# Routed token rows that carry their own token number and weights, in a mixture-of-experts stage on one core

## The chip, the cores and the metric

One core of a Trainium2 chip runs the whole kernel: a cross attention, a self attention and a mixture-of-experts block (MoE), one after the other. The metric is the device time of one execution in microseconds (us), the median of several runs.

Engines are named as in the profile: PE (TensorE), DVE (VectorE), ACT (ScalarE), POOL (GpSimd), SP (SyncE, which here only issues DMAs). An engine executes its own instructions in order, and a wait holds up everything behind it on that engine.

## The reference, cut to what matters

```python
# x: (8, 128, 512) after two attention blocks; E = 8 experts, F = 1024
def ffn(x, Wg, Wu, Wd, W1, W2):
    xt = x.reshape(1024, 512)
    probs = softmax(xt @ Wg)
    topv, topi = top_k(probs, 2)
    topv = topv / sum(topv, axis=-1)            # two weights per token
    cw = zeros((1024, 8)).at[arange(1024)[:, None], topi].set(topv)
    h = gelu(einsum('td,edf->tef', xt, Wu))
    y = einsum('tef,efd->ted', h, Wd)
    moe = einsum('ted,te->td', y, cw)
    return gelu(xt @ W1) @ W2 + moe
x = x + ffn(layernorm(x), ...)
```

Only two of the eight experts count for each token, so the kernel computes just those (2048 token and expert pairs instead of 8192).

## The kernel before, in words

The change lies in `experts()`, the last of three parts that run one after the other on all engines. Everything is float32, made of two or three passes of the faster fp32r format: a value is split into a rounded "high" part (by ACT) and a "low" rest (by DVE or POOL), and products of high and low parts are summed in PSUM.

**Tiles.** A tile is 128 rows of 512 numbers, multiplied by a pair of weight matrices (`up`, 512x1024, then GELU, then `down`, 1024x512). NT = 8 *shared* tiles (the tokens in their order, weights W1 and W2) come first. Tiles 0 to 3 of them are done in the self attention, tiles 4 to 7 in `experts()`. Then come the *routed* tiles, numbered from 8, expert after expert: each expert has the tokens that chose it, padded to whole tiles of 128. How many tiles an expert has is known only at run time (the table `first_i`); at most 31 tiles in all, and in this data 21 routed tiles, numbers 8 to 28.

**One tile** on PE, in `tile()`: 8 matmuls at each of L1728, L1732 and L1738 into `up_ps` (high x high, low x high, high x low); `turn_hidden(t, 0)` (4 transposes, L1716) as soon as ACT has made the first half of the GELU (L1799); `turn_next(t)`, the 4 transposes (L1693) of the *next* tile's rows; `turn_hidden(t, 1)`; then 8 matmuls at each of L1750, L1756 and L1760 into `down_ps`. For a shared tile the next rows are in `xn3` in SBUF; for a routed one `turn_next` first waits on `row_in`, for the DMA that fetches the row tile.

**The order of ACT's work** in `tile(t)`: two GELUs (L1799), two roundings of the transposed hidden values (L1802), the rounding of the next tile's transposed rows (`round_row`, L1785), then `load_row(t + 2)`, a DMA (L1781) of row tile t+2 from DRAM into the single buffer `row`. It can start because `rowT_done` says that the former contents of `row` have been transposed. At the start of an expert e the ACT program has `round_weights(e + 2)`, eight roundings (L1793) of the *following* expert's weights, before the GELUs of the expert's first tile.

**The order of DVE's work** in a routed tile: the low rests of the hidden values (L1848) and of the next rows (L1842); then a wait for `down_done`; then `target`, the token numbers of the tile's 128 rows (L1937), and `y`, the result times its weight (L1938), both from columns of `tag`. POOL adds `y` into the output by an indirect DMA at the rows `target` (L1646).

**Routing and scatter.** DVE finds the two experts, the weights and the slot of every token (a chain of small instructions in which each waits for the former by `link`, such as L1907; it ends with L1918, `slots_done`). Then POOL issues

- 16 indirect DMAs (8 tiles of tokens x 2 experts, L1656) that write each token's normalised row of 2048 bytes to its slot in `rows_dram`; they count on the semaphore `rows_sent`;
- 16 more (L1665) that write the pair (token number, weight), 8 bytes, to the same slot in `meta_dram`, which SP has filled with "no token, weight 0" from `pad`; they count on `added`.

Slots that no token takes must hold harmless rows: SP writes zeros from `wxo[:, 0, :]` to the 25 row tiles of `rows_dram` during the cross attention (L258 in `cross_attention`).

**Who waits for the scatter.** ACT, in `tile(NT - 2)` (tile 6), waits for `rows_sent` after `round_row(7)` and before `load_row(8)`; it then loads row tile 8, and row tile 9 in `tile(NT - 1)`. SP loads all of `meta_dram` into `tag` (L1611, `tags_in`) when `added` says that the small scatters have landed; DVE and POOL wait for `tags_in` before the routed tiles.

```python
            def tile(t, before_load=None):
                ...
                round_row(t + 1)
                if before_load:
                    before_load()
                if not isinstance(t, int) or t + 2 >= NT:
                    load_row(t + 2)
            ...
            tile(NT - 2, lambda: act.wait_ge(rows_sent, 16 * 2 * NT))
            tile(NT - 1)
```

SP's queue around this: the loads of expert 1's weights (`load_raw(2)`, 8 of 512 KB), the store of tile 6 and of tile 7, the load of `tag`, the loads of the next experts' weights.

Of the kernel before, what the change touches and what calls it, by code (L numbers as in the profile page):

```python
# [59 lines left out]
def cross_attention(nc, x_ap, ctx_ap, wq_ap, wk_ap, wv_ap, wxo_ap, q_dram, o_dram, rows_dram, wxo, wxo_in, stage, on,  # L60
# [5 lines left out]
    with ExitStack() as ctx:  # L66
# [20 lines left out]
        ones_r = sb("ones_r", [P, P], F32R)  # L87
        one = sb("one", [P, 1], F32)
# [113 lines left out]
        def _(sp):  # L202
# [45 lines left out]
            sp.wait_ge(zero_ok, 1)  # L248
            for b in range(1, B):
# [7 lines left out]
                for n in range(B * T // P + (b - 1) * ZB, min(B * T // P + b * ZB, ROWS)):  # L257
                    sp.dma_start(rows_dram[n], wxo[:, 0, :]).then_inc(zeroed, 16)  # L258
# [558 lines left out]
def self_attention(nc, x_ap, bo_ap, wxo, wxo_in, wq_ap, wkd_ap, wvd_ap, wku_ap, wvu_ap, wo_ap, wg_ap, up_ap, down_ap,  # L817
# [7 lines left out]
    with ExitStack() as ctx:  # L825
# [571 lines left out]
        def _(dve):  # L1397
# [31 lines left out]
            def norm(s, n):  # L1429
# [3 lines left out]
                nc.vector.tensor_scalar(xn3[:, s, :], x2[:, s, :], mv[:, par, 0:1], rstd[:, par, :], ALU.subtract,  # L1433
# [55 lines left out]
def experts(nc, room, stage, on, up_ap, down_ap, out_ap, rows_dram, meta_dram, x2, xn3, logits, hu0, hd0, lu0, ld0,  # L1489
# [7 lines left out]
    with ExitStack() as ctx:  # L1497
# [16 lines left out]
        row, y, g = room[:, 0, :], room[:, 1, :], room[:, 2:4, :]  # L1514
        token = sb("token", [P, NT])
        tags = sb("tags", [P, 2, NT, 2])
        pad = sb("pad", [P, MAX_TILES, 2])
        hold = sb("hold3", [P, MAX_TILES + 1])
        target = sb("target", [P, 1], U32)
        tag = sb("tag", [P, MAX_TILES + 1, 2])  # L1520
# [10 lines left out]
        hit = sb("hit", [P, 2, NT, E])  # L1531
        both = sb("both", [P, NT, E])
        rank = sb("rank", [P, NT, E])
# [22 lines left out]
        rows_sent = sem("rows_sent")  # L1556
# [12 lines left out]
        padded = sem("padded")  # L1569
        tags_in = sem("tags_in")  # L1570
# [19 lines left out]
        def _(sp):  # L1590
# [12 lines left out]
            sp.wait_ge(tags_set, 1)  # L1603
            sp.dma_start(meta_dram.rearrange("(p r) w -> p r w", p=P), pad[:, :, :]).then_inc(padded, 16)
# [12 lines left out]
        def _(pool):  # L1617
# [34 lines left out]

            pool.wait_ge(slots_done, 1)
            for t in range(NT):
                for k in range(2):
# [352 lines left out]
```

## Time and profile before

| | |
|---|---|
| Time, median of 3 runs | 1626.52 us (1625.01 to 1626.78) |
| The profiled execution | 1637.39 us |
| Its span, first to last instruction | 1635.5 us |
| Busy in the span | PE 95%, PEld (weight load) 75%, POOL 44%, ACT 42%, DVE 39% |
| Granted TensorE clock, mean | 0.983 |
| `experts()` | about 1281 to 1635.5 us |

Times in the views are us from the start of the span. A row of the timeline gives the start, the duration, engine, line, operation, output and inputs, a count, and in brackets how long the engine had been idle and what ended that. "ACTq" and the like are an engine's sequencer, which issues DMAs. The profiled execution took 10.9 us more than the median; the profile doesn't say where.

### The profile page before, as it was taken

The page shows a single profiled execution, that of the slowest core. Times are in us where ns is not written, and L with a number is a line of the kernel's source. Part 1 is how long each engine was busy: PE and PEld are TensorE (multiplying, and loading weights), DVE is VectorE, ACT ScalarE, POOL GpSimd, SP SyncE. Part 2 cuts the span into 40 slices and gives each one's busy share as a digit, 9 for nine tenths or more (in the row PEclk, how much of TensorE's full clock was granted, in tenths as well). Part 3 has the DMA queues.
Part 4 walks back from the last instruction along what each step waited for, and adds up shares of the span by engine and source line. Part 5 has one row for each costly group of instructions (what it writes and reads, how often), then busy time and mean ns, then how long its engine had stood idle before and what let it go on. Part 6 is the DMA issues. An engine that isn't in the chain of part 4 may idle for free. (4 is left out here: it accounts for less than half of the span.)

```text
span 1635.5 us, 25132 instructions
## 1 busy us (share of the span) xinstructions
PE 1560.3 (95%) x10022; PEld 1225.8 (75%) x10023; DVE 630.8 (39%) x951; ACT 694.3 (42%) x1132; POOL 722.9 (44%) x563
## 2 busy tenths in 40 slices
PE   7999999999999999999999999789899969999997
PEld 5677877877878878877877877734467747877876
DVE  4135435434434533533633632641644522222222
ACT  3244544544544544544544543414344403453522
POOL 3113913922931931941841850436200175588651
PEclk9999999999999999999999999999999989999999
DMA  5111021021021021020020110051000465556521
GB/s 206 58 52 59 1 85 57 3 84 44 16 85 33 27 85 33 27 84 31 29 85 26 33 66 27 1 205 64 23 1 1 149 212 135 149 160 191 158 39 35
DMA packets 56164, 116.90 MB, mean 71 GB/s; under 512 B 11072, under 2 KB 15232, under 8 KB 56064
## 3 DMA queue, kind: packets, MB, share of 16 engines
q1 hardware_dynamic: 46480, 98.17, 18.2%
q0 software_dynamic: 4816, 8.41, 2.7%
q10 hardware_dynamic: 4768, 8.91, 1.8%
q8 instruction: 71, 1.16, 0.3%
q14 instruction: 29, 0.24, 0.0%
HBM read 94.19 MB, written 22.33 MB: 71 GB/s over the span
## 5 line engine op out<-in xcount | busy, mean ns | idle before, releaser
L281 POOL TENSOR_TENSOR ctx_l<-stage,ctx_h 128x1024 fp32r<-128x1024 f32 x62 | 147.1, 2393 | 505.4 <-ACT ctx_h L616 505.3
L343 PE MATMUL ps_p<-wv,ctx_h 128*128 128x512 f32 x1024 | 329.3, 403 | 9.5 <-DVE ctx_l L686 9.3
L343 PE MATMUL ps_p<-ctx_h,wk 128*128 128x512 f32 x1024 | 336.2, 397 | 0.0
L724 DVE TENSOR_TENSOR s_top<-ps_s,s_top 128x512 f32<-128x512 f32 x192 | 123.5, 685 | 348.2 <-ACT s L589 348.2
L343 PEld LDWEIGHTS ps_p<-wv,ctx_h 128*128 128x128 f32 x1024 | 185.1, 189 | 56.2 <-issue 10.0
L343 PEld LDWEIGHTS ps_p<-ctx_h,wk 128*128 128x128 f32 x1024 | 192.2, 188 | 44.6 <-issue 2.9
L343 PE MATMUL ps_p<-wv,ctx_l 128*128 128x512 f32 x512 | 201.1, 393 | 0.0
L343 PE MATMUL ps_p<-ctx_l,wk 128*128 128x512 f32 x512 | 199.7, 390 | 0.0
L571 ACT ACTIVATE vt<-ps_p 128x512 f32<-128x512 f32 x128 | 76.4, 597 | 260.6 <-PE ps_p L343 199.4
L565 ACT ACTIVATE kT<-ps_p 128x512 f32<-128x512 f32 x128 | 76.4, 597 | 225.9 <-PE ps_p L343 142.3
L589 ACT ACTIVATE s<-ps_s 128x512 f32<-128x512 f32 x256 | 138.1, 598 | 52.2 <-PE ps_s L396 52.2
L396 PEld LDWEIGHTS ps_s<-qT,kT 64*128 64x128 f32 x2048 | 123.6, 187 | 38.6 <-issue 38.6
L396 PE MATMUL ps_s<-qT,kT 64*128 64x128 f32 x2048 | 146.6, 284 | 0.0
L596 ACT ACTIVATE s<-s 128x1024 f32<-128x1024 f32 x128 | 125.8, 1050 | 5.9 <-DVE s L754 5.9
L726 DVE COPY s_top<-ps_s 128x512 f32<-128x512 f32 x64 | 41.2, 686 | 208.0 <-ACT s L589 208.0
L425 PE MATMUL ps_o<-s,vt 128*64 128x128 f32 x2048 | 116.1, 276 | 0.0
L425 PEld LDWEIGHTS ps_o<-s,vt 128*64 128x64 f32 x2048 | 113.9, 139 | 2.8 <-issue 2.7
L343 PEld LDWEIGHTS ps_p<-wv,ctx_l 128*128 128x128 f32 x512 | 96.5, 189 | 21.3
L343 PEld LDWEIGHTS ps_p<-ctx_l,wk 128*128 128x128 f32 x512 | 96.2, 188 | 19.8 <-issue 1.7
L754 DVE TENSOR_TENSOR s<-s,ps_s 128x2048 f32<-128x2048 f32 x48 | 106.1, 2275 | 0.0
L1799 ACT ACTIVATE wxo<-up_ps 128x512 f32<-128x512 f32 x50 | 29.6, 598 | 179.6 <-PE up_ps L1738 155.6
L1848 DVE TENSOR_TENSOR gT_l<-gT_ps,gT_h 128x512 fp32r<-128x512 f32 x50 | 34.4, 691 | 155.3 <-ACT gT_h L1802 155.2
(252 smaller groups left out, 2291.7 us busy)
## 6 DMA issues: line engine op xcount, KB each, us to landing
stage<-in_ctx_dram SPq DMA_DIRECT2D x64, 512.0 KB, 3.9
raw_u<-in_up_dram SPq DMA_DIRECT2D x32, 512.0 KB
stage<-in_down_dram SPq DMA_DIRECT2D x16, 512.0 KB
raw_e<-in_down_dram SPq DMA_DIRECT2D x16, 512.0 KB
rows_scratch<-wxo SPq DMA_DIRECT2D x25, 256.0 KB, 2.6
wxo<-rows_scratch ACTq DMA_DIRECT2D x23, 256.0 KB
s<-in_x_dram SPq DMA_DIRECT2D x2, 1024.0 KB, 11.1
q_scratch<-s SPq DMA_DIRECT2D x2, 1024.0 KB, 4.5
```

The source lines that it names most:

```text
L281: nc.gpsimd.tensor_tensor(lo, raw, hi, ALU.subtract).then_inc(done, 1)
L343: mm = nc.tensor.matmul(out, w(c), m(c), start=(c + k == 0), stop=(c == DC - 1 and k == 2))
L396: mm = nc.tensor.matmul(ps_e[:, 2 * (n % 2) + e, i], kT[rows, p, i * P:(i + 1) * P], qT[rows, p, :], start=True, stop=True)
L425: mm = nc.tensor.matmul(ps_o[e * XD:(e + 1) * XD, p, :], vt[:, (b * MT + t) % RING, h * XD:(h + 1) * XD], s[:, h, t, :], start=(t == 0), s ...
L565: nc.scalar.activation(kT[:, p, :], ps_p[:, NTH[b, "K", g, p] % 2], ACT.Copy).then_inc(k_copied, 1)
L571: nc.scalar.activation(vt[:, nth_v(b, g, t) % RING, :], ps_p[:, NTH[b, "V", g, t] % 2], ACT.Copy) \
L589: nc.scalar.activation(s[:, 2 * p + e, 4 * g:4 * g + 4, :], ps_e[:, 2 * (n % 2) + e], ACT.Copy) \
L596: nc.scalar.activation(part, part, ACT.Exp, scale=X_SCALE).then_inc(exp_done, 1)
L724: ins = nc.vector.tensor_tensor(top[:, p, e], bank, top[:, p, e], ALU.max)
L726: ins = nc.vector.tensor_copy(top[:, p, e], bank)
L754: nc.vector.tensor_tensor(s[:, h], s[:, h], largest_score, ALU.subtract).then_inc(shifted, 1)
L1848: nc.vector.tensor_tensor(gT_l[:, 4 * n:4 * n + 4, :], gT_ps[:, n], gT_h[:, 4 * n:4 * n + 4, :], ALU.subtract).then_inc(gTl_done, 1)
```

## The change

Each row of `rows_dram` gets four more columns (`WIDE` = 516): token number, first weight, second weight and first expert. They stand in four more columns of `xn3`, so the scatter of the rows takes them along, and `meta_dram`, its 16 scatters, its filling and its load are gone. Because a slot doesn't know whether it is its token's first or second choice, DVE picks the weight per tile by comparing the first expert with the loop's e. The empty slots come from a `blank` row with the token number 1024. The first two routed row tiles are loaded by SP, ahead of the stores of tiles 6 and 7; ACT doesn't wait for the scatter any more. Before `row` is overwritten by the next load, DVE has to have copied its four columns (`take_tags`), so each `load_row` of ACT has a new wait on `tag_taken`.

```diff
+TOKEN, FIRST, SECOND, EXPERT, WIDE = D, D + 1, D + 2, D + 3, D + 4
@@ cross_attention: SP, POOL
-                    sp.dma_start(rows_dram[n], wxo[:, 0, :]).then_inc(zeroed, 16)
+                    sp.dma_start(rows_dram[n], blank[:, :]).then_inc(zeroed, 16)
-            pool.memset(wxo[:, 0, :], 0.0).then_inc(zero_ok, 1)
+            pool.memset(blank[:, :], 0.0).then_inc(zero_ok, 1)
+            pool.wait_ge(zero_ok, 1)
+            pool.memset(blank[:, TOKEN:TOKEN + 1], float(B * T)).then_inc(zero_ok, 1)
@@ experts: buffers
-        row, y, g = room[:, 0, :], room[:, 1, :], room[:, 2:4, :]
+        row = sb("row", [P, WIDE])
+        y, g = room[:, 1, :], room[:, 2:4, :]
@@ experts: SP
             load_raw(1)
-            sp.wait_ge(tags_set, 1)
-            sp.dma_start(meta_dram.rearrange("(p r) w -> p r w", p=P), pad[:, :, :]).then_inc(padded, 16)
             for t in range(NT - 2):
                 store_out(t)
             load_raw(2)
-            for t in range(NT - 2, NT):
-                store_out(t)
             sp.wait_ge(added, 16 * 2 * NT)
-            sp.dma_start(tag[:, 0:MAX_TILES, :], meta_dram.rearrange("(r p) w -> p r w", p=P)).then_inc(tags_in, 16)
+            sp.dma_start(row[:, :], rows_dram[NT]).then_inc(row_in, 16)
+            store_out(NT - 2)
+            sp.wait_ge(rowT_done, NT + 1)
+            sp.wait_ge(tag_taken, NT + 1)
+            sp.dma_start(row[:, :], rows_dram[NT + 1]).then_inc(row_in, 16)
+            store_out(NT - 1)
@@ experts: POOL
                         out_offset=bass.IndirectOffsetOnAxis(ap=slot_i[:, k, t:t + 1], axis=0),
-                        in_=xn3[:, t, :], in_offset=None).then_inc(rows_sent, 16)
-            pool.wait_ge(tags_set, 2)
-            pool.wait_ge(padded, 16)
-            for t in range(NT):
-                for k in range(2):
-                    pool.indirect_dma_start(
-                        out=meta_dram, out_offset=bass.IndirectOffsetOnAxis(ap=slot_i[:, k, t:t + 1], axis=0),
-                        in_=tags[:, k, t, :], in_offset=None).then_inc(added, 16)
+                        in_=xn3[:, t, :], in_offset=None).then_inc(added, 16)
             pool.wait_ge(firsts_done, 1)
-            pool.wait_ge(tags_in, 16)
             pool.wait_ge(out_stored, 16 * NT)
@@ experts: ACT
             def load_row(n):
+                act.wait_ge(tag_taken, n)
                 act.dma_start(row[:, :], rows_dram[bass.ds(n, 1)].rearrange("o p d -> (o p) d")).then_inc(row_in, 16)
...
-                if not isinstance(t, int) or t + 2 >= NT:
+                if not isinstance(t, int):
                     load_row(t + 2)
-            tile(NT - 2, lambda: act.wait_ge(rows_sent, 16 * 2 * NT))
@@ experts: DVE
+            def take_tags(n):
+                nc.vector.tensor_copy(tag[:, bass.ds(n, 1), :].rearrange("p o w -> p (o w)"), row[:, TOKEN:WIDE]) \
+                    .then_inc(tag_taken, 1)
+            def choose_weight(t, e):
+                dve.wait_ge(tag_taken, t + 1)
+                same, other = chosen[:, 0:1], chosen[:, 1:2]
+                nc.vector.tensor_tensor(same, of_tile(t, EXPERT), iota[:, bass.ds(e, 1)], ALU.is_equal).then_inc(choice, 1)
+                dve.wait_ge(choice, t * 3 + 1)
+                nc.vector.scalar_tensor_tensor(out=other, in0=of_tile(t, SECOND), scalar=same, in1=of_tile(t, SECOND),
+                                               op0=ALU.mult, op1=ALU.subtract).then_inc(choice, 1)
+                dve.wait_ge(choice, t * 3 + 2)
+                nc.vector.scalar_tensor_tensor(out=chosen[:, 2:3], in0=of_tile(t, FIRST), scalar=same, in1=other,
+                                               op0=ALU.mult, op1=ALU.subtract).then_inc(choice, 1)
-            for k in range(2):
-                link(nc.vector.tensor_copy(tags[:, k, :, 0].bitcast(U32), token[:, :]))
-                ins = nc.vector.tensor_copy(tags[:, k, :, 1], weight[:, :, k])
-            ins.then_inc(tags_set, 1)
+            nc.vector.tensor_copy(xn3[:, :, TOKEN], token[:, :])
+            nc.vector.tensor_copy(xn3[:, :, EXPERT], index_f[:, :, 0])
+            nc.vector.tensor_copy(xn3[:, :, FIRST:EXPERT], weight[:, :, :]).then_inc(tags_set, 1)
@@ experts: DVE, each routed tile (tile NT - 1 takes the tags of tile NT likewise)
                     hidden_rest(t)
                     row_rest(t + 1)
+                    choose_weight(t, e)
+                    dve.wait_ge(row_in, t * 16 + 32)
+                    take_tags(t + 1)
                     dve.wait_ge(down_done, t + 1)
                     dve.wait_ge(added, t * 16 + NT * 16)
-                    dve.wait_ge(tags_in, 16)
-                    nc.vector.tensor_copy(target[:, :], tag[:, bass.ds(t, 1), 0:1].rearrange("p o w -> p (o w)").bitcast(U32))
-                    nc.vector.tensor_scalar(y[:, :], down_ps[:, :], tag[:, bass.ds(t, 1), 1:2].rearrange("p o w -> p (o w)"),
-                                            None, ALU.mult).then_inc(y_copied, 1)
+                    nc.vector.tensor_copy(target[:, :], of_tile(t, TOKEN))
+                    dve.wait_ge(choice, t * 3 + 3)
+                    nc.vector.tensor_scalar(y[:, :], down_ps[:, :], chosen[:, 2:3], None, ALU.mult).then_inc(y_copied, 1)
@@ perceiver_block
-    rows_dram = nc.dram_tensor("rows_scratch", (ROWS, P, D), F32, kind="Internal").ap()
+    rows_dram = nc.dram_tensor("rows_scratch", (ROWS, P, WIDE), F32, kind="Internal").ap()
-        xn3 = ctx.enter_context(nc.sbuf_tensor("xn3", [P, B, D], F32))
+        xn3 = ctx.enter_context(nc.sbuf_tensor("xn3", [P, B, WIDE], F32))
```

## Rows read from the trace of the kernel before

**Rows 1.** The page: busy time of each engine, share of the span, instructions.

```profile
PE 1560.3 (95%) x10022; PEld 1225.8 (75%) x10023; DVE 630.8 (39%) x951; ACT 694.3 (42%) x1132; POOL 722.9 (44%) x563
```

**Rows 2.** The chain that ended last, 1318 to 1352 us: start, us, what.

```profile
1332.62 5.48 another core or an unknown queue
...
1338.72 5.73 another core or an unknown queue
...
1345.08 5.68 another core or an unknown queue
```

**Rows 3.** The timeline of PE, tiles 6 and 7.

```profile
1318.61 0.60 PE L1693 MATMUL rowT_ps<-on,xn 128*128 128x128 f32 x4
...
1319.60 2.08 PE L1750 MATMUL down_ps<-hd,gT_h 128*128 128x512 f32 x8
...
1328.76 1.97 PE L1738 MATMUL up_ps<-lu,rowT_h 128*128 128x512 f32 x8
...
1351.52 3.75 PE L1750 MATMUL down_ps<-hd,gT_h 128*128 128x512 f32 x8 [5.28 <-ACT gT_h L1802]
```

**Rows 4.** The timeline of ACT's sequencer: the first two loads of a row tile.

```profile
1332.27 0.35 ACTq L1781 DMA_DIRECT2D wxo<-rows_scratch  x1
...
1350.91 0.35 ACTq L1781 DMA_DIRECT2D wxo<-rows_scratch  x1
```

**Rows 5.** POOL's scatters: large (by tile), small (by line), last small one (timeline).

```profile
L1656 POOL DMA_INDIRECT rows_scratch<-xn,slot_i x16: 956/961/1968, 1303.0 to 1325.8; - x16
...
L1665 POOL DMA_INDIRECT meta_scratch<-tags,slot_i x16 | 15.3, 958 | 4.9 <-issue 4.9
...
1345.97 0.95 POOL L1665 DMA_INDIRECT meta_scratch<-tags,slot_i  x1 [0.30 <-issue]
```

**Rows 6.** DMA queues (packets, MB, share): 1300:1310, 1332.2:1337 and 1350.5:1354.1.

```profile
q0 software_dynamic: 234, 0.77, 20.1%
...
q10 hardware_dynamic: 124, 0.24, 59.1%
...
q10 hardware_dynamic: 144, 0.26, 25.1%
```

**Rows 7.** The timelines of ACT and DVE around the start of expert 1 (tile 11).

```profile
1391.56 0.34 ACTq L1781 DMA_DIRECT2D wxo<-rows_scratch  x1
...
1392.64 3.90 ACT L1793 ACTIVATE hu<-raw_u 128x1024 fp32r<-128x1024 f32 x4 [0.22 <-issue]
1397.15 2.01 ACT L1793 ACTIVATE hd<-stage 128x1024 fp32r<-128x1024 f32 x2 [0.61 <-PE down_ps L1760]
1399.07 1.99 ACT L1793 ACTIVATE hd<-raw_e 128x1024 fp32r<-128x1024 f32 x2
1401.65 0.60 ACT L1799 ACTIVATE wxo<-up_ps 128x512 f32<-128x512 f32 x1 [0.59 <-PE up_ps L1738]
...
1392.57 0.68 DVE L1842 TENSOR_TENSOR rowT_l<-rowT_ps,rowT_h 128x512 fp32r<-128x512 f32 x1
1397.35 0.16 DVE L1937 COPY target<-tag 128x1 uint32 x1 [4.10 <-PE down_ps L1760]
```

**Rows 8.** The timeline of DVE: eight small instructions, each linked to the former.

```profile
1298.88 1.96 DVE L1907 TENSOR_SCALAR first<-n_tiles,first 128x1 f32<-128x1 f32 x8
```

**Rows 9.** ACT's timeline and the chain: start of expert 3; last row, of expert 1.

```profile
1455.27 3.90 ACT L1793 ACTIVATE hu<-raw_u 128x1024 fp32r<-128x1024 f32 x4 [0.21 <-issue]
...
1465.75 1.09 ACT L1799 ACTIVATE wxo<-up_ps 128x512 f32<-128x512 f32 x2 [0.18 <-issue]
...
1467.93 1.98 PE down_ps L1750 x8
...
1403.87 1.31 PE down_ps L1750 x5
```

**Rows 10.** Windows, one tile each: us, busy us and count of each engine, clock, DMA.

```profile
1384.65:1397.35 12.70, 12.70 (x61) 10.22 (x60) 2.85 (x5) 6.87 (x10) 3.77 (x3) 1.00 0.53 143
...
1409.78:1422.20 12.42, 12.42 (x62) 10.22 (x61) 2.86 (x6) 2.77 (x5) 11.21 (x7) 1.00 0.79 208
```

More of the change, by code:

```diff
@@ L87, in cross_attention @@
         ones_r = sb("ones_r", [P, P], F32R)
+        blank = sb("blank", [P, WIDE], F32)
         one = sb("one", [P, 1], F32)
@@ L247, in _ @@
             sp.wait_ge(q_stored, 16 * 2)
[L248 removed]
+            sp.wait_ge(zero_ok, 2)
             for b in range(1, B):
@@ L1432, in norm @@
                 dve.wait_ge(rstd_done, n + 1)
-                nc.vector.tensor_scalar(xn3[:, s, :], x2[:, s, :], mv[:, par, 0:1], rstd[:, par, :], ALU.subtract,
+                nc.vector.tensor_scalar(xn3[:, s, 0:D], x2[:, s, :], mv[:, par, 0:1], rstd[:, par, :], ALU.subtract,
                                         ALU.mult).then_inc(xn_done, 1)
@@ L1486, in _, with experts @@
                 copy(nc.vector.tensor_copy(logits[:, s, :], bank(f"lg{s}")[:, 0:E]), f"lg{s}")
-def experts(nc, room, stage, on, up_ap, down_ap, out_ap, rows_dram, meta_dram, x2, xn3, logits, hu0, hd0, lu0, ld0,
+def experts(nc, room, stage, on, up_ap, down_ap, out_ap, rows_dram, x2, xn3, logits, hu0, hd0, lu0, ld0,
             rowT_h, rowT_l, gT_h, gT_l, raw_in, hi_done, lo_done):
@@ L1513, in experts @@
         ident, before, ones = on[:, 0, :], on[:, 1, :], on[:, 2, :]
-        row, y, g = room[:, 0, :], room[:, 1, :], room[:, 2:4, :]
+        row = sb("row", [P, WIDE])
+        y, g = room[:, 1, :], room[:, 2:4, :]
         token = sb("token", [P, NT])
-        tags = sb("tags", [P, 2, NT, 2])
-        pad = sb("pad", [P, MAX_TILES, 2])
+        chosen = sb("chosen", [P, 3])
         hold = sb("hold3", [P, MAX_TILES + 1])
         target = sb("target", [P, 1], U32)
-        tag = sb("tag", [P, MAX_TILES + 1, 2])
+        tag = sb("tag", [P, MAX_TILES + 2, 4])
         iota = sb("iota", [P, E])
@@ L1530, in experts @@
         weight = sb("weight", [P, NT, 2])
-        hit = sb("hit", [P, 2, NT, E])
-        both = sb("both", [P, NT, E])
-        rank = sb("rank", [P, NT, E])
+        room_at = lambda i, n: room[:, 0, i * NT * E:(i + n) * NT * E].rearrange("p (k t e) -> p k t e", k=n, t=NT)
+        hit, both, rank = room_at(0, 2), room_at(2, 1)[:, 0], room_at(3, 1)[:, 0]
         earlier = sb("earlier", [P, NT + 1, E])
@@ L1555, in experts @@
         firsts_done = sem("firsts_done")
-        rows_sent = sem("rows_sent")
+        tag_taken = sem("tag_taken")
+        choice = sem("choice")
         row_in = sem("row_in")
@@ L1681, in _ @@
             pool.wait_ge(row_in, end * 16 + 32)
-            pool.wait_ge(rows_sent, 16 * 2 * NT)
             pool.wait_ge(added, end * 16 + NT * 16)
@@ L1794, in round_weights, with tile @@
                         .then_inc(hi_done, 1)
-            def tile(t, before_load=None):
+            def tile(t):
                 for n in range(NH):
@@ L1817, in _ @@
             round_weights(1, None)
-            for t in range(EARLY + 1, NT - 2):
+            for t in range(EARLY + 1, NT):
                 tile(t)
-            tile(NT - 2, lambda: act.wait_ge(rows_sent, 16 * 2 * NT))
-            tile(NT - 1)
             act.wait_ge(firsts_done, 1)
@@ L1865, in _ @@
             link(nc.vector.tensor_tensor(probs[:, :, :], logits[:, :, :], spread(lmax[:, :]), ALU.subtract))
-            nc.vector.memset(pad[:, :, 1:2], 0.0)
-            nc.vector.memset(pad[:, :, 0:1].bitcast(U32), B * T).then_inc(tags_set, 1)
+            dve.sem_inc(tag_taken, NT)
+            dve.sem_inc(choice, 3 * NT)
             row_rest(EARLY)
@@ L1927, in _ @@
                 row_rest(t + 1)
+                if t + 1 == NT:
+                    dve.wait_ge(row_in, 16 * NT + 16)
+                    take_tags(NT)
                 add_shared(t)
@@ L1945, in perceiver_block @@
     o_dram = nc.dram_tensor("o_scratch", (B, P, PAIRS, T), F32, kind="Internal").ap()
-    meta_dram = nc.dram_tensor("meta_scratch", (MAX_TILES * P, 2), F32, kind="Internal").ap()
-    rows_dram = nc.dram_tensor("rows_scratch", (ROWS, P, D), F32, kind="Internal").ap()
+    rows_dram = nc.dram_tensor("rows_scratch", (ROWS, P, WIDE), F32, kind="Internal").ap()
     with ExitStack() as ctx:
@@ L1973, in perceiver_block @@
                        o_early, stage, on, x2, xn3, logits, hu, hd, lu, ld, rowT_h, rowT_l, gT_h, gT_l, raw_in, hi_done, lo_done, one)
-        experts(nc, wxo, stage, on, up, down, out, rows_dram, meta_dram, x2, xn3, logits, hu, hd, lu, ld,
+        experts(nc, wxo, stage, on, up, down, out, rows_dram, x2, xn3, logits, hu, hd, lu, ld,
                 rowT_h, rowT_l, gT_h, gT_l, raw_in, hi_done, lo_done)
```

7 lines of the change are left out of this document (3 added, 4 removed).

## The prediction, made blind

> **What bounds the kernel now.** The page shows PE busy 95% of the span [rows 1], so time can be won only where PE stands still or is made to. Read next the chain that ended last: over the routed tiles it runs along PE, except for one hole that ends at 1350.8 us [rows 2]. PE's timeline gives its size. The first `down` matmul of tile 6 starts at 1319.60 and that of tile 7 at 1351.52, 31.92 us later [rows 3]; an undisturbed tile of this weight set takes 12.42 [rows 10]. That is 19.5 us, and the eight matmuls then take 3.75 instead of 2.08 [rows 3]: 1.7 more, 21.2 us in all.
>
> What fills the hole? ACT, whose GELU PE needs, waits for `rows_sent` until 1332.27, when it issues the load of row tile 8 [rows 4]. Then the chain has three stretches of 5.5, 5.7 and 5.7 us that it puts to "another core or an unknown queue" [rows 2]: PE's matmuls had ended by 1330.7 [rows 3], yet ACT acts on them only at 1338.1, 1344.5 and 1350.8. In this time POOL issues the small scatters, the last at 1345.97 [rows 5]. No instruction of the program asks for these three stretches.
>
> **How much of the hole is there without a profile?** The profiled execution took 10.9 us more than the median (1637.4 against 1626.5). By program order alone tile 7 would wait only for the scatter and then row tile 8. That load was issued at 1332.27 and had 124 of its 144 packets by 1337 [rows 4, 6], the rest by about 1338.1. From the transpose of the next rows to the first `down` matmul it is 1.0 us [rows 3], so `down` would start at about 1339.2 instead of 1332.0 (1319.6 + 12.4): 7.2 us late, with up to 1.7 for the half clock 7 to 9. The recorded 21.2 less 10.9 is 10.3, nearly the same. I take it that most of the excess sits here, and that an ordinary execution loses 10.3 us.
>
> **The change, part by part.**
>
> *ACT's wait goes, SP loads row tile 8.* What is late next is that row tile itself: PE's `turn_next(7)` still needs it, and the rows still land at 1332.3. A quiet load of this size takes 2.4 to 3.2 us (issued at 1350.91, its 144 packets all moved by 1354.1 [rows 4, 6]); the one beside the small scatters took 5.8. I take 3.3, nearer the quiet one, because the small scatters are gone but expert 1's weights are just ending: in at 1335.6, `down` at 1336.7, 4.7 late, plus 0.9 (half of the 1.7) for the clock, since PE rests for 4 us. Rest of the hole: 5.6 us; bounds 3.8 (2.4 us and no clock loss) and 8.9 (5.8 us and all of it). Gain 21.2 - 5.6 = 15.6 in the profile's time, and 10.3 - 5.6 = 4.7 on the median.
>
> *Wider rows.* The scatter moves 0.8% more bytes. Its packets now carry 0.77 MB / 234 = 3.3 KB on average [rows 6], more than one row of 2048 bytes. The Trainium skill (DMA: Bandwidth & Descriptors, "SWDGE vs HWDGE vs iDMA") says that a packet is preferably at most 4096 bytes; two rows of 2064 no longer fit, so packets would be halved, and by its arbitration in turns per packet the scatter would get less beside the weight load. I bound it by rows: the last big scatter is issued at 1325.8 and all have landed 6.5 us later, at 1332.3 [rows 4, 5]; between no change and a third more I take none, as the bytes are all but the same, and keep 2 us for the upper bound, which is then 10.9.
>
> *16 small scatters, `pad` and the load of `tag` go.* POOL's 15.3 + 4.9 = 20.2 us [rows 5] stand beside PE's hole and nobody waits for POOL; it then waits for the last store of a shared tile. Worth nothing beyond the above. The blank rows (25 DMAs) and two memsets lie under the cross attention: 0. On DVE two links fewer in the routing, 0.5 us, before a wait for PE: 0.
>
> *Four DVE instructions per routed tile.* DVE is idle for 4.10 us before L1937 [rows 7]. Linked small instructions come every 1.96 / 8 = 0.245 us [rows 8]: 3 x 0.245 + 0.16 = 0.9 us, hidden 21 times.
>
> *The new wait before `load_row`.* Here cover is missing. ACT issued the load at 1391.56, while its own row rounding ran. Now it waits for `take_tags(t + 1)`, behind L1842 (ends 1392.57 + 0.68 = 1393.25) and the three linked instructions: 1393.25 + 0.9 + about 0.1 for the signal = 1394.25, so 2.7 us later. In most tiles ACT then rests for 9 us, and the row has 12 us to arrive. But at the start of an expert `round_weights` stands behind the load: `hu` begins at 1392.64 + 2.7 = 1395.3; the eight roundings take 3.90 + 3.91 = 7.8 without a gap [rows 7], to 1403.15; the GELU follows 0.18 later [rows 9] at 1403.3 instead of 1401.65. PE pays this in full: GELU to `down` is 2.2 us both in an ordinary tile (1401.65 to 1403.87) and after a late GELU (1465.75 to 1467.93) [rows 7, 9]. So 1.65 us at the start of expert 1, and as much at two others of its kind (2 and 5). Three more (3, 4, 6) were already late for the last piece of `raw_e`: 1455.27 + 2.7 + 7.8 + 0.18 = 1465.95 against 1465.75 [rows 9], 0.2 each. Expert 0's follows an integer tile without a load, expert 7 has none. Sum 3 x 1.65 + 3 x 0.2 = 5.5 us. Bounds: no link cost beyond issue (2.3 us later) gives 3 x 1.25 = 3.8; a register computation before each wait (3.2 later) gives 3 x 2.15 + 3 x 0.6 = 8.2.
>
> *Addresses.* Experts with the second weight set take 12.70 us a tile, those with the first 12.42 [rows 10], the clock full in both. The larger `xn3` shifts both sets by the same 128 bytes per partition. I take 0; if the second set became fast, 10 tiles gain 2.8 us; if the first became slow, 15 tiles lose 4.2.
>
> **Sum.** Against the profiled execution: 1637.4 - 15.6 + 5.5 = 1627.3. On the median: 1626.5 - 4.7 + 5.5 = 1627.3, since the excess goes with the hole. I forecast 1627.3 us, no measurable change (a difference under 0.2%, 3.3 us, can't be told from none).
>
> **The rivals.**
> - *The whole hole is real (chance 0.28).* For: ACT did stand still in it, and the small scatters are issued in most of this time (to 1346.9 of 1350.8). Against: the 10.9 us must then lie elsewhere, though PE's cadence is even. Then 1626.5 - 15.6 + 5.5 = 1616.4.
> - *Half of the excess belongs to every profile (0.13).* Then the hole is 16 us on the median: 1626.5 - (16 - 5.6) + 5.5 = 1621.6. The Trainium skill (Runtime: NRT & Kernel Launch, "The ~15µs preamble/postamble breakdown") puts about 6.2 us between a profile's total and the plain time of any kernel; an estimate by it would be 1621. No row shows it: of the 10.9, 1.9 lie outside the span.
> - *Slower: the wait on `tag_taken` costs more than the gate gives (0.21).* Place: the six expert starts. With its upper price 8.2 and a gain of 3.0 (the hole's rest at 7.3 of 10.3), it is 1631.7; it decides as soon as the gain falls 3.3 us below the price, for instance when row tile 8 again takes 5.8 us.
> - *The hole doesn't go (0.03).* PE's late signals come from the big scatter and the weight load, not from the small ones: 1626.5 + 5.5 = 1632.
>
> **How the numbers follow.** The forecast has 0.35, its own range 1624 to 1631. Faster by over 0.2%: 0.28, 0.11 of the half case and 0.03 of the forecast's (the wait at its lower price, the row at once) = 0.42. Slower: 0.18 of the third rival's 0.21, 0.03 of the last, 0.05 of the forecast's = 0.26. Same: 0.32. The range reaches from the first rival with a little of its gain's bound (1615) to the slower ones (1632).
>
> **What would show it.** Right: no wait of ACT before tile 7; PE's hole there about 5 us, ended by the row load; no stretch of an unknown queue; the row loads of ACT 2.7 us later after L1785; `hu` idle before it 2.9 instead of 0.2 at expert starts, "PE gT_ps <- ACT wxo" grown by some 5 us; profiled time and median a few us apart. Wrong: a profile still 10 us above the median (the first rivals), gaps before GELUs unchanged (the price of the wait), tiles of 12.7 in every expert (addresses).

## The result and the profile after

The changed kernel takes **1645.98 us**, median of 4 (1645.27 to 1646.73), beside 1626.65 us (1625.01 to 1627.98) of the kernel before on the same chip: ratio 1.0119, 95% interval 1.0102 to 1.0137. It is slower by 19.3 us, and lies outside the predicted range. The profiled execution took 1646.11 us with a span of 1644.3. Where one execution of a group was far longer than the rest (3951.72 us in run 6, and 5416.44 in the kernel before beside runs 6, 7, 9 and 13), the medians, ranges and ratios here leave it out.

The page's row of engine totals, beside [rows 1]: PE is busy 4.9 us more, DVE 54.7 us more. The changed kernel has 82 more DVE instructions.

```profile
PE 1565.2 (95%) x10022; PEld 1230.5 (75%) x10023; DVE 685.5 (42%) x1033; ACT 692.1 (42%) x1132; POOL 707.0 (43%) x548
```

**The hole before tile 7.** The chain that ended last of the changed kernel (start, us, what), beside [rows 2], and PE's timeline, beside [rows 3]:

```profile
1327.55 6.74 DMA rows_scratch<-xn,slot_i
1334.31 2.88 DMA row<-rows_scratch
1337.23 1.12 PE rowT_ps L1689 x4
```

```profile
1337.23 1.12 PE L1689 MATMUL rowT_ps<-on,row 128*128 128x128 f32 x4 [4.23 <-DMA row<-rows_scratch]
...
1338.85 2.68 PE L1746 MATMUL down_ps<-hd,gT_h 128*128 128x512 f32 x8
```

The stretches of an unknown queue are gone. What is left is the end of the scatter, a row load of 2.9 us, and 4.23 us in which PE stands still. The first eight `down` matmuls take 2.68 us where the profile of before had 3.75.

**The starts of the experts.** The rest of the changed kernel's profile is one story, told here at expert 3, whose first tile is late. First DVE's timeline: at 1379.67 the first instruction of `choose_weight` in an undisturbed tile, then the same instruction in the last tile of expert 2:

```profile
1379.67 0.15 DVE L1849 TENSOR_TENSOR chosen<-tag,iota 128x1 f32 x1
...
1444.45 0.68 DVE L1834 TENSOR_TENSOR rowT_l<-rowT_ps,rowT_h 128x512 fp32r<-128x512 f32 x1
1445.05 4.61 DVE L1849 TENSOR_TENSOR chosen<-tag,iota 128x1 f32 x1
1449.80 0.22 DVE L1851 SCALAR_TENSOR_TENSOR chosen<-tag,chosen 128x1 f32 x1
1450.16 0.22 DVE L1854 SCALAR_TENSOR_TENSOR chosen<-tag,chosen 128x1 f32<-128x1 f32 x1
1450.39 0.17 DVE L1839 COPY tag<-row 128x4 f32 x1
```

The timeline of POOL at that time:

```profile
1444.29 5.34 POOL L1644 TENSOR_TENSOR ld<-raw_e,hd 128x1024 fp32r<-128x1024 f32 x2
```

The timeline of ACT and its sequencer:

```profile
1443.71 0.59 ACT L1782 ACTIVATE rowT_h<-rowT_ps 128x512 fp32r<-128x512 f32 x1
1450.72 0.34 ACTq L1778 DMA_DIRECT2D row<-rows_scratch  x1
1451.79 3.90 ACT L1790 ACTIVATE hu<-raw_u 128x1024 fp32r<-128x1024 f32 x4 [7.49 <-issue]
1455.60 1.99 ACT L1790 ACTIVATE hd<-stage 128x1024 fp32r<-128x1024 f32 x2
1457.49 1.99 ACT L1790 ACTIVATE hd<-raw_e 128x1024 fp32r<-128x1024 f32 x2
1459.38 1.05 ACT L1796 ACTIVATE wxo<-up_ps 128x512 f32<-128x512 f32 x2
```

The timeline of PE:

```profile
1443.10 2.10 PE L1746 MATMUL down_ps<-hd,gT_h 128*128 128x512 f32 x8
...
1460.01 1.12 PE L1712 MATMUL gT_ps<-on,wxo 128*128 128x128 f32 x4 [5.61 <-ACT wxo L1796]
...
1462.48 2.32 PE L1746 MATMUL down_ps<-hd,gT_h 128*128 128x512 f32 x8
```

Read them from the top. An instruction on one element a partition, 0.15 us elsewhere, takes 4.61 us, all of it inside POOL's `TENSOR_TENSOR`s, and it ends at 1449.66, just after the last of POOL's row of them at 1449.63. `take_tags` stands behind it, ACT's row load waits for `tag_taken` until 1450.72, the roundings begin 1.07 later and need 7.6 us, the GELU follows at 1459.38. From the `down` of one tile to that of the next it is 19.4 us. The clock adds its part: windows over this stretch (us, busy us and count of each engine, granted clock, DMA):

```profile
1448.90:1459.90 11.00, 5.50 (x25) 4.19 (x23) 2.23 (x6) 8.11 (x10) 8.45 (x6) 0.98 0.60 176
1459.90:1464.00 4.10, 3.99 (x18) 3.75 (x19) 1.20 (x2) 2.22 (x5) 3.37 (x2) 0.62 0.69 236
```

After PE's 5.6 us of rest the granted clock is 0.62 in the next 4.1 us, a mix of both levels (1.2 and 2.4 GHz), and from the GELU to the `down` it is 3.1 us where [rows 7, 9] have 2.2.

How often, and how much? The instruction L1849 (ns: lowest, median, highest), and three rows of the waits (us in total, times, longest):

```profile
L1849 DVE TENSOR_TENSOR chosen<-tag,iota x21: 147/243/5148, 1354.0 to 1632.5; 128x1 f32 x21
```

```profile
DVE target L1953 <- PE down_ps L1756: 31.6, 11, 4.1
ACT hu L1790 <- issue: 31.5, 6, 7.6
PE gT_ps L1712 <- ACT wxo L1796: 20.3, 6, 5.8
```

In ten of the 21 tiles L1849 takes 2.88 to 5.15 us, but only three of these stand right before an expert's start (experts 3, 4 and 6); after the other seven the next tile on PE is at most 0.1 us longer.

The table below gives the periods of the tiles that matter, from the end of one tile's last `down` matmul to that of the next, read from PE's timeline of each kernel's profile. The first row is a second profiled execution of the kernel before (the first experiment).

| kernel | tile 7 | start of expert 1 | 2 | 3 | 4 | 5 | 6 |
|---|---|---|---|---|---|---|---|
| before, second execution | 23.31 | 12.43 | 12.70 | 13.81 | 14.19 | 12.46 | 14.19 |
| after | 18.05 | 13.95 | 13.99 | 19.50 | 20.56 | 13.79 | 20.54 |
| e11_take_columns | 19.79 | 13.90 | 14.10 | 14.09 | 14.26 | 13.89 | 14.27 |
| e13_pool_short | 19.69 | 13.82 | 14.04 | 13.80 | 14.05 | 13.83 | 14.04 |
| e10_act_takes | 19.38 | 12.48 | 12.70 | 13.62 | 14.05 | 12.47 | 14.07 |

The hole gave back 5.3 us. The six starts cost 22.5 us more: 1.52 + 1.29 + 1.33 = 4.1 at experts 1, 2 and 5, and 5.69 + 6.37 + 6.35 = 18.4 at 3, 4 and 6. The stages before the routed tiles were 1.9 us longer in this execution than in the other (1302.3 against 1300.4 at the end of tile 4), which varies from run to run: 1298.1 to 1302.3 over all kernels here. Together -5.3 + 22.5 + 1.9 = 19.1, and the spans differ by 1644.3 - 1624.8 = 19.5. Experts 3, 4 and 6 are those whose forerunner has only two tiles: POOL's eight roundings of about 2.9 us, begun in the forerunner's first tile, then still run when DVE comes to `choose_weight` in its last.

### The profile page after: what moved, and what is told of

The parts are those of the page before. It is cut to its first block and busy times, and to the rows that moved or that the text cites. A ratio compares the mean times of both kernels' runs of the same rounds, so it can differ in the third digit from the quotient of the medians.

```text
span 1644.3 us, 25325 instructions
## 1 busy us (share of the span) xinstructions
PE 1565.2 (95%) x10022; PEld 1230.5 (75%) x10023; DVE 685.5 (42%) x1033; ACT 692.1 (42%) x1132; POOL 707.0 (43%) x548
```

## The experiments

The theory after the first look: DVE's small instructions are held while POOL's long `TENSOR_TENSOR` runs, and the price is paid through ACT's wait. The rivals: the wait costs that much however short the instructions are; the kernel before varies by itself; the wider rows are at fault.

**Run 1 (e1_before_again): the kernel before, profiled again.** No edit.

> The kernel before, unchanged, to see whether its profiled execution of 1637.4 us was an ordinary one. If the three stretches of an unknown queue belong to every execution (first rival of the prediction), tile 7 takes some 33 us again and the profiled execution lies 10 us over the median. If they don't (the forecast's reading), tile 7 takes about 12.4 + 10 us, the span is near 1625 us, and the profiled execution agrees with the median of 1626.65.

1626.63 us, span 1624.8. The chain that ended last, and PE's timeline:

```profile
1325.64 6.66 DMA rows_scratch<-xn,slot_i
1332.32 7.14 DMA wxo<-rows_scratch
```

```profile
1339.50 1.11 PE L1693 MATMUL rowT_ps<-on,wxo 128*128 128x128 f32 x4 [5.48 <-DMA wxo<-rows_scratch]
...
1341.12 3.76 PE L1750 MATMUL down_ps<-hd,gT_h 128*128 128x512 f32 x8
```

In this execution there is no unknown queue: the hole is the scatter, then a row load of 7.14 us beside the small scatters. Tile 7 takes 23.31 us, a hole of 10.9. The first profile's 10.9 us above the median belonged to that one execution.

**Run 2 (e2_take_first): `take_tags` ahead of `choose_weight`.**

```
-                    choose_weight(t, e)
                     dve.wait_ge(row_in, t * 16 + 32)
                     take_tags(t + 1)
+                    choose_weight(t, e)
```

> The changed kernel with take_tags before choose_weight in DVE's order; nothing else. Theory A (DVE's small instructions whose inputs are all in SBUF can't run while POOL has a TENSOR_TENSOR running, and take_tags and with it ACT's load and round_weights stand behind them): the copy of 128x4 comes 0.2 us after L1834 in every tile, hu starts 1 to 2 us late instead of up to 7.6, so the six late starts shrink from 27 us together to about 8 (the 4.4 of before and 3 x 1.2); about 1646.0 - 19 = 1627 us. If the copy itself is held up as the others are (one input, also in SBUF), little changes and it stays at 1646. Theory B (the price is the new wait of ACT itself, whatever stands before the copy): only the 0.9 us of the linked instructions go, 6 x 0.9 = 5 us: 1641.

1644.15 us (1639.86 to 1645.32), ratio 1.0101 (1.0078 to 1.0124). Its instruction L1839, now first in line, is the held one:

```profile
L1839 DVE COPY tag<-row x22: 157/204/5539, 1341.1 to 1631.5; 128x4 f32 x21, 128x4 f32<-128x4 f32 x1
```

L1849 behind it takes 0.15 us each time. So it is not `choose_weight` alone: whichever of these instructions comes first is held. (In the changed kernel the COPY was never held: the instruction held ahead of it let it through only when POOL had finished.)

**Run 3 (e3_one_input): the weight chosen by instructions with one tensor input.** The column of the first weight holds the difference of the two.

```
-                nc.vector.tensor_tensor(same, of_tile(t, EXPERT), iota[:, bass.ds(e, 1)], ALU.is_equal)
-                nc.vector.scalar_tensor_tensor(out=other, in0=of_tile(t, SECOND), scalar=same, ...)
-                nc.vector.scalar_tensor_tensor(out=chosen[:, 2:3], in0=of_tile(t, FIRST), scalar=same, ...)
+                nc.vector.tensor_scalar(other, of_tile(t, EXPERT), iota[:, bass.ds(e, 1)], of_tile(t, FIRST),
+                                        ALU.is_equal, ALU.mult)
+                nc.vector.tensor_scalar(chosen[:, 2:3], other, of_tile(t, SECOND), None, ALU.add)
```

> The changed kernel with the weight chosen by two TENSOR_SCALAR instructions, each with one tensor input from SBUF and its other operands as per-partition scalars (columns hold the difference of the weights and the second weight), in the same place and order. Theory A in its narrow form (two tensor inputs from SBUF are what collides with POOL): durations of 0.15 to 0.25 us throughout, and about 1646.0 - 17 = 1629 us (hu 2.4 us late as predicted). Theory A in its wide form (any DVE instruction that reads nothing from PSUM): one of the two still takes up to 5 us, 1646 us. Theory B: one linked instruction less, 6 x 0.3 = 2 us: 1644.

1641.97 us (1641.36 to 1642.47), ratio 1.0095 (1.0076 to 1.0114). Its DVE timeline in the last tile of expert 2:

```profile
1444.89 0.27 DVE L1849 TENSOR_SCALAR chosen<-tag,iota 128x1 f32 x1
1445.30 0.21 DVE L1852 TENSOR_SCALAR chosen<-chosen,tag 128x1 f32<-128x1 f32 x1
1445.53 3.93 DVE L1839 COPY tag<-row 128x4 f32 x1
```

The same moment, with POOL at work, and two instructions pass while the third is held. So either the form or the number of elements decides: the two that pass have one element a partition, the third has four.

**Run 4 (e4_no_choice): no choice at all.** Every row is weighted by its first weight; the choice between the two is left out.

```
-                    choose_weight(t, e)
...
-                    nc.vector.tensor_scalar(y[:, :], down_ps[:, :], chosen[:, 2:3], None, ALU.mult)
+                    nc.vector.tensor_scalar(y[:, :], down_ps[:, :], of_tile(t, FIRST), None, ALU.mult)
```

> The changed kernel without the choice: every row takes its token's first weight, so the rows that are their token's second choice get a wrong weight. take_tags and ACT's wait on it stay. Theory A: take_tags follows L1834 at once, hu is 1 to 2 us late; about 1627 us. Theory B: the wait stays, so the time stays above 1640.

1640.41 us (1640.12 to 1641.91), ratio 1.0086 (1.0068 to 1.0105). The COPY of the tags alone, held for up to 4.66 us, is enough: 13.9 us above the kernel before. That is the time rival B gave (above 1640), but not for its reason: the wait is long because the COPY is held.

**Run 5 (e9_take_scaled): the COPY replaced by a `TENSOR_SCALAR`**, with run 3's choice.

```
-                nc.vector.tensor_copy(tag[:, bass.ds(n, 1), :]..., row[:, TOKEN:WIDE])
+                nc.vector.tensor_scalar(tag[:, bass.ds(n, 1), :]..., row[:, TOKEN:WIDE], iota[:, 1:2], None, ALU.mult)
```

> The changed kernel with both suspects replaced: the weight chosen by the two TENSOR_SCALARs of e3_one_input, and the tags taken from the row by a TENSOR_SCALAR (the row's four columns times a one of iota) in place of the COPY. Theory A (it is the form of the DVE instruction that POOL's long TENSOR_TENSORs hold up: a COPY and instructions with two SBUF tensor inputs are held, a TENSOR_SCALAR with scalars by pointer is not): no DVE instruction of 1 us or more among the four, expert starts 3, 4 and 6 back at about 14 us a tile, and the sum that the forecast made holds: 1626 to 1629 us. Rival B (the wait on tag_taken costs its 3 to 8 us however short the instructions are, by queueing or signal time): over 1640 us. Between the two (a TENSOR_SCALAR of four columns is held too): 1636 to 1642.

1641.50 us (1638.35 to 1643.42), ratio 1.0083 (1.0061 to 1.0105): theory A failed, and the case in between, that a `TENSOR_SCALAR` of four columns is held too, came (1636 to 1642 expected). Two of its lines (ns: lowest, median, highest):

```profile
L1849 DVE TENSOR_SCALAR chosen<-tag,iota x21: 262/265/268, 1353.6 to 1629.7; 128x1 f32 x21
```

```profile
L1839 DVE TENSOR_SCALAR tag<-row,iota x22: 221/1091/3907, 1339.4 to 1630.3; 128x4 f32 x21, 128x4 f32<-128x4 f32 x1
```

The same operation passes on one element a partition and is held on four. My reason for the form, that a `TENSOR_SCALAR` passes, was wrong.

**Runs 6 and 7 (e11_take_columns, e12_take_strided): is it the number of elements, the layout, or the source?** Both with run 3's choice. Run 6:

```
-                nc.vector.tensor_copy(tag[:, bass.ds(n, 1), :]..., row[:, TOKEN:WIDE])
+                for column in range(TOKEN, WIDE):
+                    nc.vector.tensor_copy(of_tile(n, column), row[:, column:column + 1])
```

> e3_one_input with the copy of the tags split into four COPYs of one column each, still ahead of ACT's load. In e9_take_scaled the two TENSOR_SCALARs of one column ran at 0.21 to 0.27 us beside POOL's TENSOR_TENSOR, and the one of four columns right behind them was held for 2 to 4 us; so was the COPY of four columns. Theory A (what is held is an instruction from SBUF to SBUF of several elements a partition, besides those with two SBUF inputs; one of one element and one input passes): the four take 0.06 to 0.2 us each whatever POOL does, tag_taken comes 2.7 to 3.4 us later than the load of before was issued, expert starts 3, 4 and 6 stay under 15 us, 1625 to 1629 us. Rival B (what is held is reading from row, or the COPY as such): at least one of the four is held, 1638 to 1643 us.

Run 7:

```
-        tag = sb("tag", [P, MAX_TILES + 2, 4])
+        tag = sb("tag", [P, 4, MAX_TILES + 2])
-                nc.vector.tensor_copy(tag[:, bass.ds(n, 1), :]..., row[:, TOKEN:WIDE])
+                nc.vector.tensor_copy(tag[:, :, bass.ds(n, 1)]..., row[:, TOKEN:WIDE])
```

> e3_one_input with tag laid out column by column, so that the COPY of four columns writes elements 100 bytes or more apart and not side by side. Theory A (a copy is held for the fast form that side-by-side fp32 elements allow): it is no longer held, 0.17 us in every tile, 1625 to 1629 us. Theory B (it is held for having several elements, in any layout): held for 2 to 4 us as in e3_one_input, 1638 to 1643 us.

Run 6: 1628.01 us (1624.78 to 1629.93), ratio 1.0013 (1.0003 to 1.0023). Run 7: 1640.10 us, ratio 1.0088 (1.0065 to 1.0110). The line of run 6, then that of run 7:

```profile
L1840 DVE COPY tag<-row x88: 145/154/157, 1341.4 to 1617.4; 128x1 f32 x84, 128x1 f32<-128x1 f32 x4
```

```profile
L1839 DVE COPY tag<-row x22: 159/1076/3914, 1340.6 to 1628.7; 128x4 f32 x21, 128x4 f32<-128x4 f32 x1
```

Four COPYs of one column pass beside POOL and give back 13.4 us: run 3 lay 15.4 above its kernel before, run 6 lies 2.0 above; one COPY of four columns is held, whether it writes them side by side or 132 bytes apart.

**Run 8 (e13_pool_short): is POOL the holder?** The changed kernel, nothing edited on DVE or ACT; POOL rounds 64 of each chunk's 1024 columns, and the other low parts stay those of an earlier expert.

```
-                    nc.gpsimd.tensor_tensor(weight_chunk(lu..., ld..., i), raw_part(i), weight_chunk(hu..., hd..., i), ...)
+                    few = lambda chunk: chunk[:, 0:64]
+                    nc.gpsimd.tensor_tensor(few(weight_chunk(lu..., ld..., i)), few(raw_part(i)), few(...), ...)
```

> The changed kernel as it is, but POOL rounds only the first 64 of each chunk's 1024 columns of the low weight parts in the routed tiles (the rest of lu and ld keeps the values of the expert two before, so that part is left out of the sum). Nothing on DVE or ACT is edited. Theory A (each held instruction ends when one of POOL's long TENSOR_TENSORs ends; POOL holds them): no DVE instruction of choose_weight or take_tags takes 1 us, the expert starts cost about 1.4 us at 1, 2 and 5, and at 3, 4 and 6 that or less, since raw_e comes free earlier: hole at 5.6 to 7.4 and six starts of 0 to 1.7, 1621 to 1629 us. Rival B (they are held by something else at an expert start, the weight DMAs or ACT's roundings): held as before, 1640 us or more.

1626.01 us (1622.98 to 1627.62), ratio 1.0002 (0.9991 to 1.0012). The same instruction as in the changed kernel (L1849 there), and what PE then waits for:

```profile
L1850 DVE TENSOR_TENSOR chosen<-tag,iota x21: 150/150/150, 1352.9 to 1612.3; 128x1 f32 x21
```

```profile
PE gT_ps L1713 <- ACT wxo L1797: 7.0, 6, 1.2
```

From up to 5.1 us to 0.15 in all 21 tiles, and 20 us back: POOL's instructions are the holder. That is shown.

**Run 9 (e5_before_plus3): does a held instruction cost without a waiter on ACT?** The kernel before, with three instructions of `choose_weight`'s forms ahead of the wait for `down_done`, on constants.

```
                     row_rest(t + 1)
+                    small_three(t, e)
                     dve.wait_ge(down_done, t + 1)
```

> The kernel before with three small DVE instructions per routed tile of the forms of choose_weight (two SBUF inputs), at the same place, with nothing behind them but the wait for the matmuls and y; ACT's load waits for nothing new. Theory A (a held instruction costs only through who waits for it): the first of the three is held for up to 5 us at expert starts, yet the time is that of the kernel before, 1625 to 1629 us. Rival B (held instructions, or POOL slowed by them, cost time without any waiter): 1632 us or more.

1631.58 us (1628.62 to 1633.39), ratio 1.0037 (1.0024 to 1.0049), 5.6 above its kernel before: neither expectation. Starts 3, 4 and 6 take 16.62, 14.58 and 17.57 us. The chain shows why:

```profile
1431.52 4.36 DVE chosen L1850
...
1436.64 0.76 DVE wxo L1953
...
1439.65 10.07 POOL ld L1641 x4
1449.74 4.10 DMA raw_e<-in_down_dram
1453.86 0.28 ACT hd L1795
```

A held instruction makes `y` late, `y` makes POOL's scatter late, and with it POOL's roundings, which free `raw_e` for the load that ACT needs. Two paths lead from DVE to the GELU; ACT's wait was the dearer. By the periods of the starts this one costs 2.8 + 0.4 + 3.4 = 6.6 us.

**Runs 10 and 11 (e6_before_gate, e7_before_gate_hold): the other half, the gate alone.** Run 10 is the kernel before with SP, not ACT, loading row tiles 8 and 9:

```
+            sp.wait_ge(rows_sent, 16 * 2 * NT)
+            sp.dma_start(row[:, :], rows_dram[NT]).then_inc(row_in, 16)
...
-                if before_load:
-                    before_load()
```

> The kernel before with one part of the change alone: SP, not ACT, waits for the scatters and loads row tiles 8 and 9; the small scatters, pad and the tag load stay. Theory A (in ordinary executions the hole is the row load itself, 7.1 us beside the small scatters against 2.9 without them): the hole stays at about 10 us and the time within 2 us of the kernel before, 1625 to 1628 us. Rival B (the hole was ACT standing in its own wait): the hole goes to about 5.6 and the time to 1621 to 1622 us.

Run 11 adds one wait on POOL, so that the small scatters come after row tile 8:

```
+            pool.wait_ge(row_in, 16 * NT + 16)
             for t in range(NT):
                 for k in range(2):
                     pool.indirect_dma_start(out=meta_dram, ...
```

> e6_before_gate, and POOL holds the small scatters back until row tile 8 is in. Theory A: the row load then takes about 3 us, as in the changed kernel, the hole is about 5.6 us: 1621 to 1623 us, with tags by the old way and so without any wait of ACT on DVE. Rival B (the hole is not the neighbourhood of the small scatters, but the end of the large ones or the clock): as e6_before_gate, 1625 to 1628 us. If the held scatters and the tag load come too late for tile 8's y, 1 to 5 us more.

Run 10: 1626.81 us, ratio 0.9995 (0.9982 to 1.0009), tile 7 at 23.70 us. The gate by itself gives nothing. Run 11: 1629.14 us, ratio 1.0010 (0.9999 to 1.0022). Tile 7 takes 17.80 us, so the small scatters are what the row load suffers from; but tile 9 takes 19.36. Its waits:

```profile
DVE target L1937 <- DMA out_dram<-wxo,target: 22.8, 2, 13.8
```

POOL issues its last small scatter at 1355.6, waits for the tags until 1366.6, and starts expert 2's roundings and the first scatter of `y` that much later. This price, 6.7 us at tile 9 and 1.3 at tile 10, is more than the 5.5 us of the hole. Holding the small scatters back in this way doesn't pay; the changed kernel does away with them. No other order was tried.

**Runs 12 and 13 (e8_tags_by_sp, e10_act_takes): the change without DVE in ACT's way.** Both with run 3's choice. In run 12 one DMA of SP loads the tag columns of all row tiles, behind its two row loads; `take_tags` and ACT's wait go:

```
+            sp.dma_start(tag[:, NT:MAX_TILES, :],
+                         rows_dram[NT:MAX_TILES, :, TOKEN:WIDE].rearrange("n p w -> p n w")).then_inc(tag_taken, 16)
...
-                act.wait_ge(tag_taken, n)
```

> The changed kernel, but SP loads the tag columns of all row tiles with one DMA once the scatters have landed (behind its two row loads), so that no instruction takes them from a row and ACT's loads don't wait for tag_taken; the weight is chosen by two TENSOR_SCALARs. Theory A: the whole price of the change was ACT's wait for DVE; without it the expert starts are those of the kernel before (excess 4.4 us in all), the hole at tile 7 stays at 5.6 us: 1626.6 - 10.3 + 5.6 = 1621.9, 1620 to 1624 us. Rival B (choosing the weight on DVE or the wider rows cost time by themselves, or the many 16-byte pieces of the tag load hold the row loads up): 1627 us or more.

In run 13 ACT copies the tags itself, ahead of its load:

```
+                    nc.scalar.activation(tag[:, bass.ds(t + 1, 1), :]..., row[:, TOKEN:WIDE], ACT.Copy) \
+                        .then_inc(tag_taken, 1)
```

> The changed kernel with the tags copied by ACT itself, right ahead of its load of the next row but one (an ACTIVATE Copy of four columns instead of the wait on DVE); the weight is chosen by two TENSOR_SCALARs. Theory A: ACT's copy doesn't meet POOL, costs about 0.2 us of ACT per tile, at six expert starts on the way to the GELU (1.2 us in all): 1626.6 - 10.3 + 5.6 + 1.2 = 1623.1, 1621 to 1625 us, close to e8_tags_by_sp. Rival B (the wider row, or a second cause at expert starts, costs too): 1627 us or more. If ACT's small copy is held by POOL as DVE's is: 1640.

Run 12: **1623.01 us** (1619.13 to 1624.39), ratio 0.9971 (0.9958 to 0.9984). Run 13: **1620.84 us** (1617.87 to 1624.83), ratio 0.9974 (0.9960 to 0.9988). Both beat the changed kernel, and the kernel before by about 0.3%; between them the difference can't be told. Both have the wide rows, so these cost nothing that shows, and that rival falls. ACT's copy of the same four columns in run 13, and PE's wait:

```profile
L1802 ACT ACTIVATE tag<-row x22: 206/208/210, 1336.0 to 1605.7; 128x4 f32 x21, 128x4 f32<-128x4 f32 x1
```

```profile
PE gT_ps L1712 <- ACT wxo L1796: 3.4, 3, 1.2
```

Never held, although 14 of the 22 copies began while one of POOL's long instructions ran. And the 0.2 us that I added at each start don't appear: experts 1, 2 and 5 start in 12.47 to 12.70 us, and the time is just under the 1621 to 1625 expected.

## Why the prediction was wrong

By its own steps:

- *The hole in an ordinary execution, 10.3 us*: right. 10.9 in run 1, 11.3 in run 10. The excess of the first profile was of that execution, so the first two rivals (the whole hole, half of the excess) fall. The wording "ACT's wait" was only half right: run 10 shows that ACT's gate as such costs nothing; the hole is the scatter and a row load that the small scatters stretch from 2.9 to 7.1 us (8.3 in run 10).
- *The rest of the hole, 5.6 us*: right, 18.05 - 12.42 = 5.6. That it fits to a tenth is luck: in the other runs with the wide rows it was 5.7 to 7.4. The row load took 2.88 us where I took 3.3, and 2.94 to 3.34 in those runs. The larger part of the difference is the clock. A window of the changed kernel from 1339 to 1343 us, then the same of run 6, whose hole is 7.4:

```profile
1339.00:1343.00 4.00, 4.00 (x17) 3.25 (x17) 1.36 (x3) 3.76 (x5) 0.00 (x0) 0.86 0.16 43
```

```profile
1339.00:1343.00 4.00, 4.00 (x12) 3.23 (x11) 1.53 (x6) 3.45 (x5) 0.00 (x0) 0.50 0.08 16
```

  In run 6 the granted clock stays at the lower level (0.50) through this window, and the first 16 `down` matmuls take 3.76 + 2.40 us; in the changed kernel it is back to 0.86 on average, and they take 2.68 + 2.00. Why it comes back sooner in some executions isn't shown.
- *Packets not cut by the wider row*: right. The DMA queues of the changed kernel, 1300 to 1310 us:

```profile
q0 software_dynamic: 95, 0.33, 8.5%
```

  0.33 MB in 95 packets is 3.5 KB each, more than one row of 2064 bytes, and the scatter's last part landed 6.74 us after its issue, 6.66 in run 1. The packet sizes in the two traces agree: 1024 packets of 4128 bytes, two rows each, where the kernel before has 1024 of 4096; they are over the 4096 bytes of my argument and yet not cut.
- *Addresses, 0*: right. Undisturbed tiles take 12.43 and 12.70 us as before. The tiles were miscounted: by the periods 11 take 12.70 us and 14 take 12.42, not 10 and 15; nothing hangs on it.
- ***Four DVE instructions per routed tile, "0.9 us, hidden 21 times"***: this step failed. Unheld they take 1.06 us (1430.94 to 1432.00 in run 8), so the length was right. But I priced them from [rows 8], a stretch in which POOL ran no `TENSOR_TENSOR`. In the routed tiles of before every DVE instruction beside POOL read PSUM or wrote one element, like the two of [rows 7]; the new forms were in no row, and I did not treat their neighbour POOL as an unknown to be bounded. What the runs showed instead: beside POOL's row of `TENSOR_TENSOR`s the first of the four lasts up to 5.15 us (0.15 in all 21 tiles of run 8, where POOL's are short), and the other three and ACT's load stand behind it.
- ***The new wait before `load_row`, 2.7 us later, 5.5 us in sum, at most 8.2***: the term of the sum that fell with it. Without the hold, in run 6, it is 4.3 at experts 1, 2 and 5 together and 0.4 at the others: 4.7 us, close to the 5.5. With the hold it is 22.5, the clock included: from GELU to `down` I took 2.2 us, and after PE's long rest it was 3.1. The slower rival had the place, the six starts, and the sign right, but its price ended at 8.2 us, about a third of what came. (Its own sum comes to 8.5: the load 0.5 us later than in the forecast adds 0.5 to the 0.2 of experts 3, 4 and 6 too, so 0.7 and not 0.6.)

Put together: 1626.6 - 5.3 + 22.5 = 1643.8 and 1.9 of ordinary variation, against 1646.0 measured.

The Trainium skill (SBUF — State Buffer, "Who interferes with whom") has the rule that I should have weighed: a DVE instruction with two SBUF inputs contends with a GpSimd instruction that reads SBUF, as do copies and `tensor_scalar`s in a two-port mode, and the second to come "fully blocks"; PE and ACT never wait. The trace agrees: DVE's instructions end with one of POOL's, and ACT's copy of the same columns is never held. It also shows more: the hold goes on through POOL's next instructions (4.61 us beside instructions of 2.4 to 3.0). The Trainium skill (VectorE: DVE Perf Modes, "What auto-detection actually checks") lets a copy within SBUF take a two-port mode when the outermost dimensions of more than one element are both even, or equal, and asks for neighbouring elements only in its 16-bit modes, which agrees with run 7; that a one-column COPY escapes is what run 6 shows. Whether the mode as such is the cause can't be read from a trace.

## What to carry to other kernels

Before you put a small instruction on DVE, look at what POOL does at that moment, not only at whether DVE is idle: a form that reads SBUF twice, or moves several elements a partition within SBUF (four here), may last until POOL's whole row of back-to-back instructions is over, not just its current one. Price it at what is left of that row, and ask who stands behind it, on its engine and through semaphores. When such an instruction must come before something urgent, give it to ACT or to a DMA, or cut it into forms that the trace shows passing.

## What was not expected of the hardware

- DVE instructions of 0.15 to 0.23 us lasted up to 5.54 us, and up to 8.18 in run 9, beside POOL's `TENSOR_TENSOR`s (2.4 to 3.0 us each): a `TENSOR_TENSOR` or `SCALAR_TENSOR_TENSOR` with both inputs in SBUF on one element, a COPY and a `TENSOR_SCALAR` on four. One-element COPYs (0.15) and `TENSOR_SCALAR`s (0.21 to 0.27) were never held.
- A held instruction waits for a gap in POOL's row, not for the end of one instruction. DVE in run 9, then POOL at that time:

```profile
1368.78 8.18 DVE L1850 TENSOR_TENSOR chosen<-iota 128x1 f32 x1
```

```profile
1366.88 5.37 POOL L1641 TENSOR_TENSOR ld<-stage,hd 128x1024 fp32r<-128x1024 f32 x2
1371.60 5.34 POOL L1641 TENSOR_TENSOR ld<-raw_e,hd 128x1024 fp32r<-128x1024 f32 x2
```

  The profile shows POOL's four overlapping by some 0.6 us each; DVE's instruction begins in the first and ends at 1376.96, just after the last (1376.94). So do the ten long ones of the changed kernel: each ends 24 to 27 ns after the last of such a row. Only in tile 8, where POOL's instructions overlap by 0.04 us, did held instructions end between two of them (L1849 after 0.24 us).
- A row load took 7.14 us beside the 16 scatters of 8-byte rows (256 KB; 8.30 in run 10), 2.88 us without them (258 KB, the changed kernel).
- One profiled execution of the kernel before took 10.9 us more than the median, 10.3 of it in tile 7 (33.65 us by PE's timeline against 23.31 in run 1), where the chain has three stretches that the profile could name no queue for; run 1 has none of them.
